# Half of the context loaded in 32 by 32 blocks and turned by VectorE instead of TensorE

## The reference

```python
def xattn(latents, context, Wq, Wk, Wv, Wo):
    hidden = concatenate([context, latents], axis=1)     # 128 + 128 keys in a batch
    q = latents @ Wq
    k = hidden @ Wk
    v = hidden @ Wv
    attn = softmax(q k^T / sqrt(128))
    return (attn v) @ Wo
x = x + xattn(layernorm(x), ctx_4096, Wq, Wk, Wv, Wo)
x = x + ffn(layernorm(x), ...)                           # sign weights, 8 soft-routed scales
```

## Time and profile before

| | us |
|---|---|
| median of 3 runs | 660.75 (660.54 to 660.89) |
| the profiled execution, whole | 660.18 |
| its span in the trace | 658.4 |
| TensorE busy in the span | 650.3 (99%) |
| VectorE, ScalarE, GpSimd busy | 483.4, 376.5, 396.3 |

### The profile page before, as it was taken

The page is one execution under the profiler, slowest core; times in us unless marked ns, Lnnn a source line. Parts: engine busy times, 40 slices in busy tenths (PEclk is TensorE's granted clock), DMA queues, the critical chain, the costliest instruction groups (busy, mean ns, idle before and its releaser), DMA issues.

```text
span 658.4 us, 11059 instructions
## 1 busy us (share of the span) xinstructions
PE 650.3 (99%) x3298; PEld 547.1 (83%) x3298; DVE 483.4 (73%) x915; ACT 376.5 (57%) x925; POOL 396.3 (60%) x315
## 2 busy tenths in 40 slices
PE   8999999999999999999999999999999999999996
PEld 6888888888888888888888888888888888878875
DVE  5652232678897889788878887888788788979866
ACT  4344242675575558555764675557556755676643
POOL 3236665287476458545954595457546759974686
PEclk9999999999999999999999999999999999999999
DMA  9656665477898787788878888887888888776612
GB/s 327 251 204 223 239 248 192 154 264 237 283 294 257 258 271 260 260 263 272 272 241 265 270 288 254 265 277 253 262 264 274 256 284 261 256 261 225 189 67 82
DMA packets 96476, 161.68 MB, mean 246 GB/s; under 512 B 9064, under 2 KB 49256, under 8 KB 95392
## 3 DMA queue, kind: packets, MB, share of 16 engines
q1 hardware_dynamic: 96416, 160.97, 74.8%
HBM read 108.38 MB, written 52.56 MB: 244 GB/s over the span
## 4 chain that ended last, share of the span: by engine, by line
PE 95%; POOL 1%; issue 1%; DVE 1%; ACT 1%; POOLq 0%; DVEq 0%
PE bank L1766 24%; PE bank L1550 23%; PE bank L1692 20%; PE bank L1731 13%; PE bank L1610 6%; PE bank L1846 2%; PE bank L1803 1%; PE bank L1747 1%; POOL wo_pair L668 1%; PE bank L1591 1%; PE bank L1567 1%; PE bank L1795 1%; PE bank L1559 1%; PE bank L1751 0%; PE bank L1818 0%
## 5 line engine op out<-in xcount | busy, mean ns | idle before, releaser
L632 POOL TENSOR_TENSOR p_low<-p_low,p_high 128x1024 fp32r<-128x1024 f32 x64 | 153.7, 2402 | 156.6 <-ACT p_high L774 156.5
L1766 PE MATMUL bank<-wo_pair,oT 128*128 128x512 f32 x720 | 175.9, 392 | 0.3 <-POOL wo_pair L668 0.3
L911 ACT ACTIVATE prob<-bank,nmax 128x256 f32<-128x256 f32 x256 | 119.0, 471 | 70.2 <-DVE nmax L1287 65.1
L1766 PEld LDWEIGHTS bank<-wo_pair,oT 128*128 128x128 f32 x720 | 131.0, 188 | 25.5 <-POOL wo_pair L668 1.0
L1550 PEld LDWEIGHTS bank<-kg,qT 128*128 128x128 f32 x768 | 107.8, 190 | 9.9 <-issue 0.2
L1287 DVE TENSOR_REDUCE nmax<-bank 128x2 f32<-128x512 f32 x128 | 87.2, 684 | 37.9 <-PE bank L1550 37.3
L1550 PE MATMUL bank<-kg,qT 128*128 128x256 f32 x768 | 111.2, 282 | 0.0
L1307 DVE STREAM_TRANSPOSE p_turned<-prob 128x512 f32<-128x512 f32 x128 | 90.0, 704 | 26.0 <-ACT prob L911 21.3
L774 ACT ACTIVATE oT<-bank 128x512 fp32r<-128x512 f32 x64 | 38.3, 598 | 111.8 <-DVE bank L1321 111.8
L1692 PE MATMUL bank<-xT,wq_ring 128*128 128x512 f32 x336 | 82.4, 391 | 0.0
L662 POOL TENSOR_TENSOR wq_ring<-raw_a,wq_ring 128x512 fp32r<-128x512 f32 x42 | 54.4, 1295 | 27.8 <-ACT wq_ring L774 27.8
(11 more groups left out here) (143 smaller groups left out, 936.3 us busy)
## 6 DMA issues: line engine op xcount, KB each, us to landing
p_park<-p_turned SPq DMA_DIRECT2D x64, 512.0 KB, 3.6
p_low<-p_park SPq DMA_DIRECT2D x64, 512.0 KB, 5.8
kg<-k_park SPq DMA_DIRECT2D x64, 256.0 KB, 3.2
vg<-v_park SPq DMA_DIRECT2D x64, 256.0 KB, 3.8
v_park<-v_stage SPq DMA_DIRECT2D x8, 1024.0 KB, 4.4
raw_a<-in_L_xattn_Wq SPq DMA_DIRECT2D x32, 256.0 KB, 5.4
raw_b<-in_L_xattn_Wo SPq DMA_DIRECT2D x32, 256.0 KB, 5.3
k_park<-k_stage SPq DMA_DIRECT2D x8, 1024.0 KB, 4.1
```

The costliest lines, as they stand in the source:

```text
L632: nc.gpsimd.tensor_tensor(part, part.bitcast(fp32), p_high[:, :].rearrange("p i c q -> p (i c q)"), ALU.subtract).then_inc(p_lo, 1)
L911: ins = nc.scalar.activation(prob[:, p, j], s_bank[p][:, j * KEYS:(j + 1) * KEYS], ACT.Exp, bias=nmax[:, p, j:j + 1], accum_out=esum[:, t ...
L1766: last = nc.tensor.matmul(wo_bank[:, :], oT[:, s, h, :], wo_pair[:, w, h, :], start=((s, w) == TERMS[0] and h == 0), stop=((s, w) == TERMS ...
```

## The change

Batches 0 to 3 of the context are treated as before. For batches 4 to 7 (`BY_TENSOR = 4` and up):

- **Loads.** They are issued behind x 2 to 7 and Wk, as four DMAs a batch instead of one. Each fills 32 partitions and gathers 32x32 blocks: a piece is 32 consecutive columns of one row, 128 bytes, and 16 pieces make up a partition's 2 KB. That is 512 pieces in a DMA and 8192 for the four batches.
- **Turning.** VectorE transposes each 32x32 block in place of the grid (`ct_turn`), from `craw[:, b]` to `craw[:, b - 4]`, where the old contents have been turned by TensorE long before. Since the DMA has put the blocks where a whole transpose needs them, the result is the turned tile. TensorE's transposes of these batches are gone.
- **HI.** `ct_half` reads `craw` in SBUF instead of the PSUM bank.
- **LO.** GpSimd subtracts (`ct_low`) in place of VectorE; `ct_low` of batches 4, 5 and 6 stands in front of `make_rstd` of batches 5, 6 and 7, that of batch 7 behind them. `ct_turn` stands where `ct_rest` stood.

```diff
+    BY_TENSOR = 4
...
             def load_c(b):
-                sp.dma_start(craw[:, b, :], ctx[b]).then_inc(c_in[b], 16)
+                if b < BY_TENSOR:
+                    sp.dma_start(craw[:, b, :], ctx[b]).then_inc(c_in[b], 16)
+                    return
+
+
+                rows = ctx[b].rearrange("(j s) (c i r) -> i s c j r", s=32, i=QB, r=32)
+                for i in range(QB):
+                    sp.dma_start(craw[32 * i:32 * i + 32, b].rearrange("s (c j r) -> s c j r", c=HC, r=32),
+                                 rows[i]).then_inc(c_in[b], 16)
...
             for b in range(2, B):
+                if b < BY_TENSOR:
+                    load_c(b)
+                load_x(b)
+            sp.dma_start(raw_b[:, :, :], wk.rearrange("(c p) n -> p c n", p=P)).then_inc(wk_in, 16)
+            for b in range(BY_TENSOR, B):
                 load_c(b)
-                load_x(b)
-                if b == 4:
-                    sp.dma_start(raw_b[:, :, :], wk.rearrange("(c p) n -> p c n", p=P)
-                                 ).then_inc(wk_in, 16)
...
+            def ct_low(b):
+
+                pool.wait_ge(ct_hi, b + 1)
+                part = cT[:, :, :, b * T:(b + 1) * T]
+                nc.gpsimd.tensor_tensor(part[:, LO], craw[:, b - BY_TENSOR].rearrange("p (c t) -> p c t", c=HC),
+                                        part[:, HI], ALU.subtract).then_inc(ct_rested, 1)
+
             for b in range(B):
+                if b > BY_TENSOR:
+                    ct_low(b - 1)
                 make_rstd(b)
+            ct_low(B - 1)
...
+                if b < BY_TENSOR:
+                    act.wait_ge(ct_ready, b + 1)
+                    turned_rows = t_bank[1][:, :]
+                else:
+                    act.wait_ge(ct_turned, b - BY_TENSOR + 1)
+                    turned_rows = craw[:, b - BY_TENSOR]
...
+            def ct_turn(b):
+
+                dve.wait_ge(c_in[b], 16 * QB)
+                dve.wait_ge(ct_ready, b - BY_TENSOR + 1)
+                nc.vector.transpose(craw[:, b - BY_TENSOR], craw[:, b]).then_inc(ct_turned, 1)
+
...
-                        (ct_rest, xt_rest)[kc](b + 1)
+                        (ct_rest if b + 1 < BY_TENSOR else ct_turn, xt_rest)[kc](b + 1)
...
-                    if a == LO:
+                    if a == LO and kc == 0 and b >= BY_TENSOR:
+                        pe.wait_ge(ct_rested, b - BY_TENSOR + 1)
+                    elif a == LO:
                         pe.wait_ge(lo_sem, b + 1)
...
-                    if b + 1 < B:
-                        (ct_transpose, xt_transpose)[kc](b + 1)
+                    if kc == 1 and b + 1 < B:
+                        xt_transpose(b + 1)
+                    elif b + 1 < BY_TENSOR:
+                        ct_transpose(b + 1)
```

More of the change, by code:

```diff
@@ L221, in xattn_ffn @@
             sem(n) for n in ("stats_ready", "mv_ready", "rstd_ready", "rstd_step", "y_ready"))
-        xt_ready, xt_hi, xt_lo, ct_ready, ct_hi, ct_lo = (
-            sem(n) for n in ("xt_ready", "xt_hi", "xt_lo", "ct_ready", "ct_hi", "ct_lo"))
+        xt_ready, xt_hi, xt_lo, ct_ready, ct_hi, ct_lo, ct_turned, ct_rested = (
+            sem(n) for n in ("xt_ready", "xt_hi", "xt_lo", "ct_ready", "ct_hi", "ct_lo", "ct_turned", "ct_rested"))
         proj_ready, proj_hi, proj_lo = sem("proj_ready"), sem("proj_hi"), sem("proj_lo")
@@ L582, in _ @@
             pool.wait_ge(proj_ready, 2 * B)
-            pool.wait_ge(ct_ready, B)
+            pool.wait_ge(ct_ready, BY_TENSOR)
+            pool.wait_ge(ct_turned, B - BY_TENSOR)
+            pool.wait_ge(ct_rested, B - BY_TENSOR)
             x_op(0, x_tmp, b12[:, HI], b12[:, LO], ALU.add)
@@ L785, in ct_half @@
             def ct_half(b):
-                act.wait_ge(ct_ready, b + 1)
-                copy(cT[:, HI, :, b * T:(b + 1) * T],
-                     t_bank[1][:, :].rearrange("p (c t) -> p c t", c=HC)).then_inc(ct_hi, 1)
+                if b < BY_TENSOR:
[4 more added lines that the diff above has]
+                    turned_rows = craw[:, b - BY_TENSOR]
+                copy(cT[:, HI, :, b * T:(b + 1) * T], turned_rows.rearrange("p (c t) -> p c t", c=HC)
+                     ).then_inc(ct_hi, 1)
             for c in range(HC):
```

## The result

The changed kernel took **668.25 us** (median of 6 runs, 666.26 to 670.16), the kernel before in the runs beside it 661.03 (660.54 to 662.01). The ratio is **1.0103**, 95% interval 1.0087 to 1.0118: 7.2 us slower, where 1.75 us faster was forecast, and 0.75 us beyond the upper end of the range. Run a second time, unaltered and on another chip, it took 667.23 us against 661.14, 1.0092 (1.0077 to 1.0107); that time lies inside the range. The profiled execution has a time of 669.8 us and a span of 668.0; before it was 658.4.

A forecast was written before the change was run, and what follows sets the result against it. TensorE was taken to bound the kernel, with the DMA queue deciding: 660.75 us less 1.75 for removed transposes, with no wait added, gave 659.0 us. The range was 658.6 to 667.5 us.

The forecast's parts named there:

- SyncE is no limit: an issue takes 0.44 us whatever the shape: SyncE's load queue: last x load issued at 10.55 us, 12 more issues end at 17 us.
- The price of a piece: DMA engines, block loads: time p per 128-byte piece, bounds 7.6 to 42.7 ns, taken as 10 ns.
- the break-even of 13.4: Piece price in ns from which TensorE's wait eats the whole 1.75 us gain.
- S: TensorE's loss in front of unit 6 from the late v_park(0) store: 512p - 5.1 us if positive, forecast 0.
- my 3.3: v_park(0) store behind the block loads: lands 2.7 + 0.6 us after its start.
- rival 1: Block loads: pieces cost 21.4 ns, TensorE waits 5.9 us at unit 6, 664.9 us; chance 0.24 to 27 ns, 0.12 beyond.
- the clock after the wait: TensorE after idling 16.8 us, at 42.7 ns a piece: whether its clock falls, no row shows; no size given.
- the deadline: v_park(0) store: may land as late as 25.7 us at no cost to unit 6; before, it landed at 24.7.
- The four sets of transposes: TensorE, context of batches 4 to 7: removing 4 x 0.44 us takes 1.75 us off the path.
- The helpers: VectorE, ScalarE, GpSimd: new work costs nothing; the case that they lose the gain, 0.9 us at worst, 659.9 us, chance 0.08.
- the chain of who waits for whom: Before unit 6: v_park(0) landing, then `v_half` on ScalarE, then `v_rest` on VectorE (0.66 us), which frees unit 6's bank.
- the contexts: Block loads: no problem; batch 4 in at 16.1 + 128p, wanted at 29.8 us; batch 7 at 16.1 + 512p, wanted about 48.

The follow-up runs named there:

- the first experiment: Block loads of batches 5, 6 and 7 issued behind the v_park stores of batches 0, 1 and 2, against the changed kernel; 659.59 us, ratio 0.9966.

## Why the prediction was wrong, and where it was right

**The step that failed** is "SyncE is no limit: an issue takes 0.44 us whatever the shape". The step was taken from one row, of whole rows of 2 KB, and the block loads have another form. They issued in 0.64 us at least, and the first five were held back by another 4.7 us in all: five of the 16 were out at 17.7 us, where I had all of them out at 17. From there on the pace was SyncE's, 0.68 us for 512 pieces, not the engines', whose 14 ns on 16 engines make 0.45 us. v_park(0) was issued at 27.21 us, 6.7 after its time. The holding back weighs more than the longer issue: with 16 at 0.68 and none held back the store would have been issued at about 21.4 by SyncE's count, 0.9 late, and there were 1.0 us of room.

The trace of the kernel before could have warned me. The issues of the four Wq loads, behind the fourth store (ns minimum/median/maximum):

```profile
L347 SPq DMA_DIRECT2D raw_a<-in_L_xattn_Wq x4: 502/760/1137, 36.7 to 39.4; - x4
```

These have 128 pieces of 2 KB each, and two of the four took over a microsecond: neither one duration for all nor 0.44.

**The price of a piece** was the step that I took for the decisive one. I took 10 ns, the measured one is 14.0 here and 12.9 with 128 partitions, on either side of the break-even of 13.4. By my own formula S would have been 512 x 14 ns - 5.1 = 2.1 us; that is what the engines alone would have cost, a small loss. The formula lets the store start at 16.1 + 7.2 + 1.2 = 24.5 and land at 27.8. It was issued 2.7 us later, which is SyncE's part, and took 2.3 us longer from there than my 3.3; with these 5.0 the wait would be 7.1, and 6.8 were measured. This split is worked out, not measured: no run issued the blocks from another engine than SyncE, which would have parted the two. The pace in the end was 0.68 us for 512 pieces on 16 engines, 21 ns a piece, which is the figure of rival 1 (21.4 ns, S = 5.9 against 6.8). That is luck: rival 1 had full engines, and they were idle for a third of the time.

**A term that the sum lacked** is the clock after the wait. The prediction said of it that no row shows it, and only for waits of 16.8 us. It fell in waits of 6.8 and 5.3 us and cost 1.9 and 3.0 us, and even in that of 2.3 us with 256 bytes, for 1.6. Rival 1 with it would have given 664.9 + 1.9 = 666.8.

**A smaller miss:** I let the store land 3.3 us after its start, and 4.2 after its issue in the earlier trace rows. It landed after 5.6 here, but after 5.6 to 5.8 also in two kernels where no block moved beside it, and after 4.2 in two others. The wait sums up so: 6.7 us of late issue, 1.4 of late landing, less the 1.0 us of room up to the deadline = 7.1, against 6.8 measured. Why some stores need 5.6 us is not settled.

**What was right.** The four sets of transposes: with whole rows to 32 partitions the key projection starts at 57.77 us, where I had 57.9, and the first experiment won 1.94 us against 1.75. The helpers: `ct_turn` took 0.70 us, `ct_low` 1.28 to 1.30, ScalarE's copy 0.63, and in the two kernels with whole rows TensorE waits for nothing in units 7 to 15; GpSimd's work in order of time, in the changed kernel:

```profile
45.99 1.30 POOL L583 TENSOR_TENSOR cT<-craw,cT 128x512 fp32r<-128x512 f32 x1 [5.62 <-ACT cT L797]
47.37 0.22 POOL L563 TENSOR_SCALAR vare<-mv 128x1 f32<-128x1 f32 x1
```

The deadline and the chain of who waits for whom, v_park, `v_half`, `v_rest`, unit 6, are as the prediction named them:

```profile
32.82 0.60 ACT L797 ACTIVATE v_stage<-bank 128x512 fp32r<-128x512 f32 x1 [7.95 <-DMA v_park<-v_stage]
```

```profile
PE bank L1646 <- DVE v_stage L1151: 6.8, 1, 6.8
```

And the contexts were never late: no wait of VectorE for `craw` in any trace.

**The range** ended at 667.5, p = 26.6 ns. The median fell 0.75 us beyond, and the second set, 667.23, inside. Without the clock's 1.9 us, as the trace has them, the first would have been inside too. The direction was wrong in both.

## What to carry to other kernels

A load that isn't urgent should not stand in front of a store that is, in a queue that works in order: the same loads between the stores turned 1.0103 into 0.9966. Cost a DMA twice, at its engines and at the sequencer that issues it, and take the issue time from a row of the same form; a row of whole rows says nothing on rows torn into pieces, nor on how long their issues are held back. Where TensorE is made to stand, reckon with what its clock may cost afterwards: 1.6 to 3.0 us in the five traces here with waits of 2.3 to 9.3 us, and nothing where dummy matmuls came first.

## What the runs showed of the hardware

- An issue of a load of whole rows took SyncE 0.42 to 0.44 us where nothing held it back, of one in several pieces a row 0.58 to 0.67, nearly the same for 256, 512 and 1024 pieces.
- The block loads issued while others were still being moved were held back, the longer the more pieces each had: the longest issue took 1.3 us with 256 pieces, 2.5 with 512 and 4.0 with 1024. Loads of whole rows took up to 0.7 us, and those of Wq, 128 pieces of 2 KB, up to 1.14.
- A packet occupied a DMA engine 10.9 ns for 64 bytes, 12.9 to 14.0 for 128 and 22 for 256. Pieces of 512 bytes moved at 296 GB/s, rows of 2 KB at 396.
- TensorE's granted clock was 0.61 and 0.71 in the two windows of 5 us that hold the end of a wait of 6.8 us and what follows, 0.69 and 0.63 in the two that hold the end of one of 5.3 us, and 1.00 throughout when dummy matmuls had left 2.6 us of waiting. With 256 bytes it was 0.95 and 0.70 around a wait of 2.3 us.
